# Attention stream: shift columns turned by fp32r matmuls from a 448-column tile instead of fp32 transposes

## The reference

```
x = x + 0.5 * ffn0(ln(x))    # dense gated FFN + 8 experts, top 2
x = x + attn0(ln(x))         # relu attention
x = x + 0.5 * ffn0(ln(x))
x = x + 0.5 * ffn1(ln(x))    # 8 experts, top 4
x = x + attn1(ln(x))         # the stage that the change touches
x = x + 0.5 * ffn1(ln(x))
```

## Time and profile before

| what | value |
|---|---|
| median of 3 runs | 536.68 us (536.38 to 537.72) |
| the profiled execution's own time | 537.0 us |
| its span, first to last instruction | 535.3 us |
| mean granted TensorE clock | 0.982 |
| matmuls and weight loads | 3074 each |

### The profile page before, as it was taken

How to read it: one execution, slowest core, us unless ns; L and a number is a source line. 1 busy time by engine, 2 the same in 40 slices (tenths; PEclk the granted TensorE clock), 3 DMA queues, 4 the chain that set the end, 5 groups by cost and what they waited for, 6 DMA issues and landing times.

```text
span 535.3 us, 9081 instructions
## 1 busy us (share of the span) xinstructions
PE 496.9 (93%) x3074; PEld 422.9 (79%) x3074; DVE 387.8 (72%) x1196; ACT 252.5 (47%) x539; POOL 109.9 (21%) x170
## 2 busy tenths in 40 slices
PE   2999999999999999999999995899788989899996
PEld 1788888888888888888888884788666778678885
DVE  4569787664786764788588679878759878638776
ACT  3657543534333434324474345355436766644441
POOL 1001000110100110100002015337503433414452
PEclk9999999999999999999999998899989999899999
DMA  6322310000000000001200000267388430000011
GB/s 205 118 90 77 100 42 1 1 1 1 2 0 1 1 1 1 2 0 41 59 21 1 1 2 1 89 73 125 121 197 262 115 96 2 2 1 1 1 40 39
DMA packets 18797, 25.87 MB, mean 48 GB/s; under 512 B 2848, under 2 KB 12832, under 8 KB 18752
## 3 DMA queue, kind: packets, MB, share of 16 engines
q1 hardware_dynamic: 17696, 24.78, 17.4%
q10 hardware_dynamic: 1056, 0.51, 0.3%
HBM read 17.42 MB, written 5.24 MB: 42 GB/s over the span
## 4 chain that ended last, share of the span: by engine, by line
PE 79%; DVE 10%; issue 3%; ACT 3%; SPq 2%; DMA 1%; POOL 1%; DVEq 0%; ACTq 0%; POOLq 0%
PE ps L578 22%; PE ps L580 21%; PE ps L579 21%; DVE x L1589 3%; PE ps L907 2%; PE ps L593 2%; PE ps L859 2%; PE ps L890 1%; PE ps L980 1%; DVE ps L1672 1%; PE ps L871 1%; DVE tmp L1432 1%; PE ps L888 1%; ACT z L1012 1%; PE ps L969 1%
## 5 line engine op out<-in xcount | busy, mean ns | idle before, releaser
L578 PE MATMUL ps<-zh,w0u_h 128*128 128x512 f32 x256 | 103.2, 403 | 1.5 <-ACT zh L1019 1.5
L580 PE MATMUL ps<-zl,w0u_h 128*128 128x512 f32 x256 | 102.5, 400 | 0.0
L579 PE MATMUL ps<-zh,w0u_l 128*128 128x512 f32 x256 | 102.1, 399 | 0.0
L1041 ACT ACTIVATE gel<-ps 128x512 f32<-128x512 f32 x64 | 38.2, 597 | 104.6 <-PE ps L580 104.5
L1407 DVE TENSOR_TENSOR act<-gel,ps 128x512 f32<-128x512 f32 x64 | 43.7, 683 | 42.5 <-ACT gel L1041 42.4
L578 PE MATMUL ps<-w0d_h,ah 128*128 128x256 f32 x256 | 73.0, 285 | 0.4
L580 PE MATMUL ps<-w0d_l,ah 128*128 128x256 f32 x256 | 71.4, 279 | 0.0
L579 PE MATMUL ps<-w0d_h,al 128*128 128x256 f32 x256 | 71.4, 279 | 0.0
L1589 DVE SCALAR_TENSOR_TENSOR x<-ps,aff,x 128x256 f32<-128x256 f32 x128 | 53.0, 476 | 9.9 <-PE ps L580 8.2
L1047 ACT ACTIVATE ah<-act 128x512 fp32r<-128x512 f32 x64 | 40.3, 629 | 40.4 <-DVE act L1407 40.4
L578 PEld LDWEIGHTS ps<-zh,w0u_h 128*128 128x128 f32 x256 | 48.7, 190 | 12.7 <-ACT zh L1019 1.8
(11 more groups left out here) (182 smaller groups left out, 1041.0 us busy)
## 6 DMA issues: line engine op xcount, KB each, us to landing
stage<-in_w_dram SPq DMA_DIRECT2D x16, 384.0 KB, 3.1
qs<-split_out SPq DMA_DIRECT2D x24, 128.0 KB, 2.8
ks<-split_out SPq DMA_DIRECT2D x48, 64.0 KB, 2.6
stage<-in_w_dram SPq DMA_DIRECT2D x8, 256.0 KB, 2.6
ks<-pad SPq DMA_DIRECT2D x6, 256.0 KB, 9.7
ks<-pad SPq DMA_DIRECT2D x1, 1024.0 KB, 9.3
split_out<-qh SPq DMA_DIRECT2D x4, 256.0 KB, 2.5
split_out<-ql SPq DMA_DIRECT2D x4, 256.0 KB, 3.0
```

The costliest lines, as they stand in the source:

```text
L578: pe.matmul(o, lh, rh, start=start, stop=False, **kw)
L579: pe.matmul(o, ll, rh, start=False, stop=False, **kw)
L580: return pe.matmul(o, lh, rl, start=False, stop=stop, **kw)
L1041: nc.scalar.activation(gel[:, n % 2, :], ps[:, 2 * (n % 2), :], ACT.Gelu_apprx_tanh).then_inc(gelu_s, 1)
```

## The change

The shift tile moves from `macc` to the first 448 columns of `pad`: 2 buffers of 224 columns (96 + 128). In a buffer the four blocks overlap: block i is the window of 128 columns that begins at 32 i, so that its last 32 columns are its own shift columns, and the 96 before them are zeros or belong to its neighbours. Rows 0 to 95 of a turned block then hold numbers that nobody reads. The turn is a matmul in fp32r, with the window as the stationary operand and an identity rounded to fp32r as the moving one; ACT makes that identity once, over the router weights that are no longer used. Both shift parts are written as fp32r. POOL now waits, before it sets the tile, until the copies out of `pad` have landed.

```diff
-        shift = macc[:, :, :].rearrange("p t d -> p (t d)").rearrange("p (s c m) -> p s c m", s=2, c=4)
...
+        ident_r = wr_h[:, 0, 0, :]
+        shift = pad[:, 0:2 * (K_ROWS + P)].rearrange("p (s m) -> p s m", s=2)
+        shift_cols = shift[:, :, K_ROWS:K_ROWS + P].rearrange("p s (c m) -> p s c m", c=4)
...
+        ident_r_s = sem("ident_rounded")
...
-                    nc.gpsimd.memset(shift[:, :, :, :], 0.0).then_inc(shz_s, 1)
+                    pool.wait_ge(zero_s, 6 * 16)
+                    pool.wait_ge(pad_s, 16)
+                    nc.gpsimd.memset(shift.bitcast(F32), 0.0).then_inc(shz_s, 1)
                     pool.wait_ge(shz_s, 1)
-                    nc.gpsimd.memset(shift[:, :, :, ONE_COL:ONE_COL + 1], 1.0).then_inc(shz_s, 1)
+                    nc.gpsimd.memset(shift_cols[:, :, :, ONE_COL - K_ROWS:ONE_COL - K_ROWS + 1].bitcast(F32), 1.0).then_inc(shz_s, 1)
...
             def shift_turn(g):
                 if g == 0:
+                    pe.wait_ge(ident_r_s, 1)
                     pe.wait_ge(shz_s, 2)
...
-                    mm = pe.transpose(ps[:, 2, i * P:(i + 1) * P], shift[:, g % 2, i, :], ident[:, :])
+                    mm = pe.matmul(ps[:, 2, i * P:(i + 1) * P], shift[:, g % 2, SLOT * i:SLOT * i + P], ident_r,
+                                   start=True, stop=True)
...
                             nc.scalar.activation(pad[K_ROWS:P, :], rows_raw, ACT.Copy).then_inc(rows_s, 1)
+                            nc.scalar.activation(ident_r, ident[:, :], ACT.Copy).then_inc(ident_r_s, 1)
...
-                cols = shift[:, g % 2, :, :]
-                return nmin[:, g % 2, :, :], cols[:, :, K_ROWS:K_ROWS + 2], cols[:, :, K_ROWS + 2:K_ROWS + 4]
+                cols = shift_cols[:, g % 2, :, :]
+                return nmin[:, g % 2, :, :], cols[:, :, 0:2], cols[:, :, 2:4]
...
-                V.tensor_copy(hi.bitcast(F32R), m).then_inc(shh_s, 1)
+                V.tensor_copy(hi, m).then_inc(shh_s, 1)
...
-                V.tensor_tensor(lo, m, hi, ALU.subtract).then_inc(shl_s, 1)
+                V.tensor_tensor(lo, m, hi.bitcast(F32), ALU.subtract).then_inc(shl_s, 1)
```

## The result

The changed kernel takes 538.31 us (median of 20 executions) against 536.36 for the kernel before (20 beside it): ratio 1.0036, 95% interval 1.0021 to 1.0052. That is slower by about 1.9 us, near the 0.3% that the prediction took for the least that can be told from no change; the interval holds that bound, but not 1. The forecast was 537.0 and no change; the measured time lies in its range, near the upper end, and its sign lies with the 0.10 for slower. Executions over 1.5% above the fastest of their kernel are left out of the ratios (here one of the 20, at 544.67 us, and further down one of nine), but not out of the medians, mean clocks and counts. The profiled execution of the changed kernel took 539.0 us, its span is 537.3.

What follows compares the result with a forecast made beforehand. TensorE was taken as the bound (busy 93% of the span, the end hanging on it for 79%). Turns +0.3 us, DVE, ACT, POOL and waits 0: 536.7 + 0.3 = 537.0 us, no change; range 534.6 to 538.6.

Steps and rivals of the forecast that it cites:

- the 0.10 for slower: Sign of the whole result: chance 0.10 (0.05 + 0.05) that the kernel gets slower by more than 0.3%.
- turn's pace: Attention stream's turns on TensorE: 115 ns each against 109, times 4, times 11 groups, +0.3 us.
- Neither bound: Limits for the turn's cost in the attention stream: 61 ns each, -2.1 us; 222 ns each, +5.0 us.
- rivals 1 and 2: Turns step by 61 ns, 534.6 us, chance 0.12; or cost 222 ns like plain fp32, 541.7 us, chance 0.05.
- That saving, counted at 0: Turn's result reaches ACT 0.05 us sooner (225 ns against 272); counted 0, bounds 0 and -0.5 us.
- POOL, ACT, the transfer: POOL's waits already satisfied, its memset halved, ACT's identity copy hidden in the 365 us gap, pad transfer unmoved: cost 0.
- rival 3: Clock: half-clock stretch like the 3.4 us one at 464.83 added or saved: 538.6 or 535.4 us, chance 0.10.

Runs made afterwards that it cites:

- the tile alone: Changed kernel's tile, POOL waits, ACT identity copy and casts, but turns as fp32 transposes again; ratio 1.0004 to the kernel before.
- wide turns: Changed kernel with three of four turns per group moving 256 columns instead of 128; ratio 1.0011 to the kernel before.
- wide 888: Changed kernel, turns left narrow, with the first matmul of the turned scores moving its 128 columns twice; ratio 1.0009 to the kernel before.
- the mirrored runs: Changed kernel with 256-column turns only in the first five groups, or only in the other eleven; ratios 1.0025 and 1.0064 to the kernel before.

## Why the prediction was right and where it was not

The **turn's pace** was right in substance. Forecast 115 ns against 109; in the trace after, the four turns of a group end about 112 ns apart at full clock, so +3 ns and not +6. In the chain a group's turns and the score behind them take 0.40 + 0.17 = 0.57 us where they took 0.44 + 0.12 = 0.56: the recorded start behind a short matmul is early here as well, so the 0.40 is no gain. Neither bound came true, and rivals 1 and 2 are out: a group still takes 3.39 us, there are 64 instructions, and no two turns end near 61 or 145 ns apart at full clock. A recorded step near 61 ns is there (56 to 62 ns from the first start to the second, where the first turn has the short duration), but it is the same early start as behind line 888. The duration of a turn did not fall to 225 ns in the median either:

```profile
L878 PE MATMUL ps<-wr_h,pad x64: 221/275/415, 400.4 to 469.0; 128*128 128x128 f32 x64
```

Only the first of the four has 221 to 224, in 12 of the 16 groups; the later ones last about 275 at full clock, so the result reaches ACT no sooner. That saving, counted at 0, was indeed 0.

The figure that the Trainium skill's page "TensorE: Matmul & The Clock Gate", section "Back-to-back issue gap", gives for a pair at N = 128 (81 ns) does not hold for these fp32r pairs: 112 ns.

**POOL, ACT, the transfer.** All as forecast; the rows after, timeline of POOL, ACT and SP and the list of transfers:

```profile
379.52 0.51 POOL L576 MEMSET pad<- 128x448 f32 x1
...
382.34 0.19 POOL L490 TENSOR_SCALAR zs_e<-mv 128x4 f32<-128x4 f32 x1 [2.14 <-DVE mv L1304]
```

```profile
365.64 0.31 ACT L1141 ACTIVATE wr_h<-ident 128x128 fp32r<-128x128 f32 x1
367.11 0.60 ACT L1125 ACTIVATE act<-ps 128x512 f32<-128x512 f32 x1 [1.15 <-PE ps L586]
```

```profile
365.64 0.58 SPq L448 DMA_DIRECT2D ks<-pad  x1
...
ks<-pad SPq DMA_DIRECT2D x1, 1024.0 KB, 8.9
```

The spread lands at 365.64 + 8.9 = 374.5, five us ahead of the memset, which starts behind the one before it without a wait, and is half as long; POOL then idles 2.14 us instead of 1.65. The identity copy takes 0.31 us and ACT still idles 1.15 us behind it. The run with the tile alone (1.0004, interval 0.9988 to 1.0020) agrees with the zeros of all three.

**The step that failed is rival 3, the clock,** in its case against: "the waits that come before it are ACT's and DVE's, which the change does not touch". It looked at the stretch at the tail alone, and only at what starts one and not at how soon one ends, and so gave 0.05 to slower. The runs show stretches of 13.6, 23.9 and, with the turns twice, 27.2 us inside the stream, with TensorE reported busy for 98.9% of each or more, where the profiles of the kernel before have 3.4 us just ahead of the first turn and none in the steady stream. The price of 1.6 us for a stretch of 3.4 us was not too small: at 2.2 us a group (5.58 - 3.39) 3.4 us in the steady stream cost some 1.3. What was mis-sized is the length, four and seven times that, and how often it comes. With 16 of 34 executions below a clock of 0.979, the median moved by 1.9 and 1.5 us instead of 0.3.

That the measured 538.31 us lies in the range is in part luck. The upper end, 538.6, was set by one more stretch of 3.4 us; the two profiled executions of the changed kernel had longer ones, one of them took 544.43 us, and the median came out lower because about half of the executions had a clock of 0.979 or more.

That wider matmuls shorten the half-clock time is shown by the clocks: with wide turns, wide 888 or both, 1 of 36 executions lies below 0.979. The stretches at the entry agree (3.4, 6.8 and 6.8 us), with one profile of each. The changed kernel was not run beside the last two, so a difference between chips is a rival there, which the low clocks of the turns issued twice and of the mirrored runs on the same chips speak against. That the fp32 transpose counts like a wide matmul because it streams its 128 columns slowly, so that it has no idle part in its pace, is argued, not shown; what fits it is that a plain fp32 instruction of 128 columns steps at 111 ns as well.

## What to carry to other kernels

Price a small matmul by the distance between the ends of several or by the time of a whole group, not by the recorded step behind it: with 128 stationary columns and 128 moving, the fp32r matmul costs 112 ns here and the fp32 transpose 109, so there was nothing to win in the swap. When a TensorE instruction is replaced by one of another type at nearly the same pace, read the granted clock run by run and look at the executions' distribution, since a single profile shows one draw from it. And where a matmul's pace hardly depends on its moving columns, extra ones can cost next to nothing (0.24 us instead of 0.23 for the turned scores' pair, about 118 ns instead of 112 for a turn) and hold the clock.

## What the runs showed of the hardware that was not expected

- Half clock was granted for 13.6, 23.9 and 27.2 us on end with PE busy for 13.43, 23.81 and 26.89 of them; being reported busy did not bring full clock back.
- Making matmuls wider, with no useful column more, brought the mean clock from 0.9773 back to 0.9821 (turns), 0.9828 (the turned scores) and 0.9843 (both).
- Extra fp32 transposes raised the mean clock (0.9870 against 0.9835 beside them), while with extra fp32r turns of the same shape it was lower (0.9692, against 0.9773 and 0.9774 for the changed kernel, which was not run beside it).
- The steady stream at half clock is slower by 5.58 / 3.39 = 1.65, not by 2. Single steps grow by more: a turn from 112 ns to 213, line 915's sixteen from 0.79 us to 1.44. The full-clock group also holds waits that the other doesn't have (line 896 once takes 0.23 us there instead of 0.06).
